# A two-layer graph network with expert layers, second stage: expert groups of two node tiles instead of four, two experts to a step, a fourth gather buffer, and inverse square roots computed on VectorE

## What is computed

```python
x = x + gnn0(layernorm(x))       # h = x @ weight_l, gathered over 100000 edges, weighted, summed by dst
x = x + experts0(layernorm(x))   # 8 experts, all applied, weighted by a softmax gate
x = x + gnn1(layernorm(x))
x = x + experts1(layernorm(x))   # 32 experts, the best one applied
# experts0, for each expert e:
h = relu(bn(x @ W1[e] + b1)); h = relu(bn(h @ W2[e] + b2)); y = h @ Wo[e] + bo; out += w[e] * y
# layernorm: (x - mean) / sqrt(var + 1e-5);  bn: g * (h - m) / sqrt(v + 1e-3) + be
```

## Time and profile before

| | |
|---|---|
| median of three executions | 2962.04 us |
| the profiled execution | 2958.48 us, its span 2956.5 us |
| TensorE busy | 2599.4 us (88%) |
| VectorE busy | 2167.4 us (73%) |
| ScalarE busy | 1565.7 us (53%) |
| GpSimd busy | 1957.5 us (66%) |
| second stage, slot 26 to 195 (577 to 1690 us) | 1113 us |
| second stage after the last edges (1690 to 1828 us) | about 138 us |

### The profile page before, as it was taken

The page is one execution under the profiler, slowest core; times in us unless marked ns, Lnnn a source line. Parts: engine busy times, 40 slices in busy tenths (PEclk is TensorE's granted clock), DMA queues, the critical chain, the costliest instruction groups (busy, mean ns, idle before and its releaser), DMA issues. The chain is left out here.

```text
span 2956.5 us, 54481 instructions
## 1 busy us (share of the span) xinstructions
PE 2599.4 (88%) x19092; PEld 2420.7 (82%) x19092; DVE 2167.4 (73%) x5110; ACT 1565.7 (53%) x3295; POOL 1957.5 (66%) x1696
## 2 busy tenths in 40 slices
PE   5799935799999999999999994599999999999999
PEld 5799825788888888888888873489999999999999
DVE  8898836577787777777878754767777777777773
ACT  4477636788888888888888762111212112121212
POOL 0355557777777877777777501877777777777770
PEclk9999956799999999999999997689999999999999
DMA  2133454332333333233233203788888888888880
GB/s 74 6 82 77 93 137 144 91 97 78 109 108 91 99 108 110 79 107 110 78 115 108 80 1 114 212 205 214 204 215 214 212 208 215 213 213 209 212 212 24
DMA packets 241962, 390.31 MB, mean 132 GB/s; under 512 B 43642, under 2 KB 115218, under 8 KB 241426
## 3 DMA queue, kind: packets, MB, share of 16 engines
q0 software_dynamic: 163072, 310.24, 41.1%
q1 hardware_dynamic: 78324, 74.90, 8.0%
q10 hardware_dynamic: 288, 1.61, 0.1%
HBM read 343.43 MB, written 43.19 MB: 131 GB/s over the span
## 5 line engine op out<-in xcount | busy, mean ns | idle before, releaser
L1409 POOL DMA_INDIRECT f_got<-h_tab,list_cols x784 | 981.1, 1251 | 291.0 <-issue 219.1
L2121 POOL DMA_INDIRECT n_got<-h_tab,edge_cols x784 | 806.5, 1029 | 238.5 <-issue 227.6
L1690 DVE TENSOR_TENSOR f_hlo<-edge_cols,f_hhi 128x1024 fp32r<-128x1024 f32 (+1 forms) x208 | 242.0, 1163 | 294.3 <-ACT f_hhi L1498 294.1
L1585 PE MATMUL bank<-f_mhi,f_hot 128*128 128x256 f32 x1168 | 329.0, 311 | 131.2 <-DVE f_mlo L1684 131.1
L1468 ACT ACTIVATE f_got<-f_got,list_cols 128x256 f32<-128x256 f32 x784 | 333.9, 497 | 145.6 <-DMA f_got<-h_tab,list_cols 145.1
L2185 ACT ACTIVATE n_hrh<-bank 128x512 fp32r<-128x512 f32 x196 | 116.9, 597 | 535.6 <-PE bank L2254 535.6
L1585 PEld LDWEIGHTS bank<-f_mhi,f_hot 128*128 128x128 f32 x1168 | 247.6, 212 | 148.0 <-issue 143.8
L1493 ACT ACTIVATE edge_cols<-bank,f_shf,f_scl 128x512 f32<-128x512 f32 (+1 forms) x416 | 295.1, 743 | 106.9 <-PE bank L1400 76.7
L2232 PE MATMUL bank<-n_got,n_hot_h 128*128 128x256 f32 x784 | 242.2, 309 | 99.4 <-DMA n_got<-h_tab,edge_cols 59.0
L1586 PE MATMUL bank<-f_mlo,f_hot 128*128 128x256 f32 x1168 | 320.3, 304 | 0.0
L400 POOL DMA_INDIRECT list<-runs,off_i x98 | 158.0, 1612 | 215.2 <-DVE off_i L759 99.0
(11 more groups left out here) (331 smaller groups left out, 7833.0 us busy)
## 6 DMA issues: line engine op xcount, KB each, us to landing
f_got<-h_tab,list_cols POOLq DMA_INDIRECT x784
n_got<-h_tab,edge_cols POOLq DMA_INDIRECT x784, 3.8
n_rows<-acc_tab SPq DMA_DIRECT2D x24, 256.0 KB, 4.7
out_rows<-n_rows SPq DMA_DIRECT2D x24, 256.0 KB, 3.7
h_tab<-acc SPq DMA_DIRECT2D x37, 128.0 KB, 3.5
edge_cols<-in_w SPq DMA_DIRECT2D x16, 256.0 KB, 2.8
acc<-in_x SPq DMA_DIRECT2D x4, 896.0 KB, 7.9
h_tab<-hbuf SPq DMA_DIRECT2D x7, 512.0 KB
```

What stands on the lines that cost most here:

```text
L1409: nc.gpsimd.indirect_dma_start(got[:, s % RING0, u, :], None, h_tab[0], bass.IndirectOffsetOnAxis(gidx0[:, s * U + u:s * U + u + 1], 0), b ...
L1585: nc.tensor.matmul(tile_bank(t), lhs, mhi[:, s % 2, u, :], start=begins, stop=False)
L1690: nc.vector.tensor_tensor(hlo[l][:, :, 0:w], rl[:, :, 0:w], hhi[l][:, :, 0:w].bitcast(F32), ALU.subtract).then_inc(s_lo[l], 1)
L2121: nc.gpsimd.indirect_dma_start(got[:, s % RING, u, :], None, h_tab[1], bass.IndirectOffsetOnAxis(gidx[:, s * U + u:s * U + u + 1], 0), bou ...
```

## The change

Groups get two tiles (`GS` = 2, 256 columns; group 0 still one), and a step takes as many experts as fill 512 columns: two (four for group 0). `layer` then issues 48 matmuls of 256 columns where it issued 24 of 512, each relu pair is four activations of 256 columns, and `hhi`, `hlo` and `add_out` keep their sizes. Four steps make a group, so that a group comes every 8 slots. Group 1 begins in slot 18, the steps of group 0 in slots 10 and 12, and the number of steps falls from 104 to 98. The rows of groups lie in six places instead of three, `rl` is two buffers, and the rows after the experts have places of their own (`before4`), which removes some waits. `RING0` is 4. The roots on ScalarE go; VectorE computes the inverse root from a first guess by bit shift and three rounds, 11 small dependent instructions where it had 5 (`inverse_root`). The same is done for the roots of the batch norm at the start.

```diff
-GS = 4
+GS = 2
+ROW_SETS = 6
...
-RING0 = 3
+RING0 = 4
...
+SEED = float(0x5f3759df)
+ROOT_STEPS = 11
...
-            xraw, rl = (edge_cols[:, b * F * W4:(b + 1) * F * W4].rearrange("p (f n) -> p f n", f=F) for b in range(2))
+            xraw, rl0 = (edge_cols[:, b * F * W4:(b + 1) * F * W4].rearrange("p (f n) -> p f n", f=F) for b in range(2))
+            rl = (rl0, sb3("rl1", [P, F, W4]))
...
+            def experts_of(g):
+                return W4 // (width(g) * P)
+
+            CUM = tuple(itertools.accumulate((EXPERTS0 // experts_of(g) for g in range(NG)), initial=0))
+            STEPS = CUM[NG]
+            GROUP_OF_STEP = [g for g in range(NG) for _ in range(CUM[g], CUM[g + 1])]
...
-                FFN.append(max(READY[g] + 5, FFN[-1] + 2 * EXPERTS0 if g else 0))
-            STEPS = NG * EXPERTS0
+                FFN.append(max(READY[g] + 5, FFN[-1] + 2 * (CUM[g] - CUM[g - 1]) if g else 0))
 
             def begin(n):
-                return FFN[n // EXPERTS0] + n % EXPERTS0 * 2
+                g = GROUP_OF_STEP[n]
+                return FFN[g] + (n - CUM[g]) * 2
+
+            def step_experts(n):
+
+                g = GROUP_OF_STEP[n]
+                per = experts_of(g)
+                return g, range((n - CUM[g]) * per, (n - CUM[g]) * per + per)
+
+            def columns(g, i):
+                return slice(i * width(g) * P, (i + 1) * width(g) * P)
...
-            DONE = [FFN[g] + 2 * EXPERTS0 + 2 for g in range(NG)]
-            NORM4 = [DONE[g] + (1 if g == NG - 1 else 2) for g in range(NG)]
+            DONE = [FFN[g] + 2 * (CUM[g + 1] - CUM[g]) + 2 for g in range(NG)]
+            NORM4 = [DONE[g] + (1 if g == NG - 1 else 3) for g in range(NG)]
             BASE = [DONE[g] + (1 if g == NG - 1 else 6) for g in range(NG)]
+            BIAS = [READY[g] + (10 if g == NG - 2 else 9) for g in range(NG)]
             UPPER = [n + 1 for n in NORM4]
             LOWER = [NORM4[g] + (1 if g == NG - 1 else 2) for g in range(NG)]
...
-                pairs = range((width(g) + 1) // 2)
-                for j in pairs:
-                    USES.append((READY[g] + 2 + j, "turn", g, j))
-                    USES.append((READY[g] + (9, 15)[j], "bias", g, j))
+                USES.append((READY[g] + 2, "turn", g, 0))
+                USES.append((BIAS[g], "bias", g, 0))
...
-                return store[g % 3][:, k, :]
+                return group_rows(g)[:, k, :]
 
             def group_rows(g, a=0, b=None):
-                return store[g % 3][:, a:width(g) if b is None else b, :]
+                at = g % 2 * GS
+                return store[g // 2 % 3][:, at + a:at + (width(g) if b is None else b), :]
 
 
 
             def before(k):
-                return (acc[:, 4, :], acc[:, 5, :], acc[:, 6, :], part[:, 6, :])[k]
-
-            def behind(j, w=2):
-                return (part, xn)[j][:, 4:4 + w, :]
+                return acc[:, 4 + k, :]
+
+            def before4(k):
+                return (acc[:, 6, :], part[:, 6, :])[k]
+
+            def behind(k):
+                return part[:, 4 + k, :]
...
-                    if l:
-                        act.wait_ge(s_lo[0], n + 1)
-                    elif n:
-                        act.wait_ge(s_lo[1], n)
+                    if n:
+                        act.wait_ge(s_lo[l], n)
                     i = 4 * n + 2 * l
                     for m in range(F):
                         act.wait_ge(s_mm[l], 2 * n + m + 1)
-                        nc.scalar.activation(rl[:, m, 0:w], bank[(i + m) % 3][:, 0:w], ACT.Relu,
-                                             bias=shf[:, l, e, m:m + 1], scale=scl[:, l, e, m:m + 1]).then_inc(s_relu, 1)
+                        for j, e in enumerate(experts):
+                            last = nc.scalar.activation(rl[l][:, m, columns(g, j)], bank[(i + m) % 3][:, columns(g, j)],
+                                                        ACT.Relu, bias=shf[:, l, e, m:m + 1], scale=scl[:, l, e, m:m + 1])
+                        last.then_inc(s_relu, 1)
                     act.wait_ge(s_relu, i + 2)
                     if n:
                         act.wait_ge(s_mm[l + 1], (2 - l) * n)
-                    nc.scalar.activation(hhi[l][:, :, 0:w], rl[:, :, 0:w], ACT.Copy).then_inc(s_hi[l], 1)
+                    nc.scalar.activation(hhi[l][:, :, :], rl[l][:, :, :], ACT.Copy).then_inc(s_hi[l], 1)
...
-                    if s - 1 in READY:
-                        g = READY.index(s - 1)
-                        t, w = tile(g, 0), width(g)
-                        act.wait_ge(s_var, t + w)
-                        nc.scalar.activation(scale[:, t:t + w], var[:, t:t + w], ACT.Sqrt).then_inc(s_sd, 1)
...
+                        for j, e in enumerate(experts):
+                            if g == 0 and m == 0:
+                                pe.wait_ge(s_wlo, 3 * e + l + 1)
+                            at = columns(g, j if l else 0)
+                            hi_x, lo_x = (hhi[0], hlo[0]) if l else (xhi, xlo)
+                            for f in range(F):
+                                last = three(bank[i % 3][:, columns(g, j)],
+                                             whi[l][:, e, f, m * P:(m + 1) * P], wlo[l][:, e, f, m * P:(m + 1) * P],
+                                             hi_x[:, f, at], lo_x[:, f, at], f == 0, f == F - 1)
...
+                    for j, e in enumerate(experts):
+                        if g == 0:
+                            pe.wait_ge(s_wlo, 3 * e + 3)
+                        for k in range(width(g)):
+                            o = j * width(g) + k
+                            for f in range(F):
+                                last = three(out_tile(o), hhi[1][:, f, o * P:(o + 1) * P], hlo[1][:, f, o * P:(o + 1) * P],
+                                             whi[2][:, e, f, :], wlo[2][:, e, f, :], f == 0, f == F - 1)
...
+                    for j, e in enumerate(experts):
+                        if e:
+                            dve.wait_ge(s_out, OUT_TILES * n + j * width(g))
+                        for k in range(width(g)):
+                            nc.vector.scalar_tensor_tensor(row(g, k), out_tile(j * width(g) + k), gate[:, g % 2, k, e:e + 1],
+                                                           row(g, k), ALU.mult, ALU.add).then_inc(s_out, 1)
+
+                def inverse_root(r, v, x, counter, base):
+
+                    bits, seed = v.bitcast(I32), r.bitcast(I32)
+                    nc.vector.tensor_scalar(x.bitcast(I32), bits, 1, None, ALU.arith_shift_right).then_inc(counter, 1)
+                    dve.wait_ge(counter, base + 1)
+                    nc.vector.tensor_scalar(seed, x.bitcast(I32), -1.0, SEED, ALU.mult, ALU.add).then_inc(counter, 1)
+                    for i in range(3):
+                        dve.wait_ge(counter, base + 3 * i + 2)
+                        nc.vector.tensor_tensor(x, r, r, ALU.mult).then_inc(counter, 1)
+                        dve.wait_ge(counter, base + 3 * i + 3)
+                        nc.vector.scalar_tensor_tensor(x, x, -0.5, v, ALU.mult, ALU.mult).then_inc(counter, 1)
+                        dve.wait_ge(counter, base + 3 * i + 4)
+                        nc.vector.scalar_tensor_tensor(r, x, 1.5, r, ALU.add, ALU.mult).then_inc(counter, 1)
+                    dve.wait_ge(counter, base + ROOT_STEPS)
...
-                        dve.wait_ge(s_sd, g + 1)
-                        newton(t, w, s_newton, 5 * g)
+                        dve.wait_ge(s_var, t + w)
+                        newton(t, w, s_newton, ROOT_STEPS * g)
                         if g:
-                            dve.wait_ge(s_made, USE_NO["turn", g - 1, (width(g - 1) - 1) // 2] + 1)
-                        split = [h for h in range(NG) if LOWER[h] <= s]
-                        if split:
-                            dve.wait_ge(s_hst, 16 * HSTORES[split[-1] + 1])
+                            dve.wait_ge(s_made, USE_NO["turn", g - 1, 0] + 1)
...
-                        dve.wait_ge(s_sd4, g + 1)
-                        newton(t, w, s_newton4, 5 * g)
+                        dve.wait_ge(s_var4, g + 1)
+                        newton(t, w, s_newton4, ROOT_STEPS * g)
                         if g:
                             dve.wait_ge(s_hst, 16 * HSTORES[g])
-                        turns = [h for h in range(NG) if READY[h] + 1 <= s]
-                        dve.wait_ge(s_made, USE_NO["turn", turns[-1], (width(turns[-1]) - 1) // 2] + 1)
                         for k in range(w):
-                            nc.vector.tensor_scalar(before(k), row(g, k), mean[:, t + k, 0:1],
+                            nc.vector.tensor_scalar(before4(k), row(g, k), mean[:, t + k, 0:1],
```

138 lines of the change are left out of this document (40 added, 98 removed).

## The result

The changed kernel takes 2957.61 us (median of 20 runs), the kernel before 2965.99 in as many: ratio **0.9972, interval 0.9962 to 0.9982, 8.4 us faster**. Forecast were 2978 us and, as the likeliest, slower by over 0.2%. The time lies in the range, the sign is wrong. The profiled execution of the changed kernel took 2956.42 us (span 2954.5), 1.2 less than its median; that of the kernel before (2958.48, span 2956.5) lies 7.5 under its own. So the two traces show only part of the gain: the gathers of the third stage start at 1833.16 us instead of 1837.29, 4.1 us earlier.

The account below looks back on a forecast made before the run. No single engine but a ring of TensorE, ScalarE and VectorE, just under the gathers' floor of 100.6 us a period. 49.7 + 5.8 + 7.4 - 41.1 - 2.9 - 3 = +15.9 gave 2978 us; range 2908 to 3022.

Parts of the forecast that it names:

- the period: 16 slots of the steps with edges: 105.5 us now, 110.2 us forecast, by waits +1.5, matmuls +1.5, clock +1.7.
- Matmuls: Two layers of a step on TensorE, 256 columns instead of 512: 5.74 us instead of 5.55, +1.5 us a period.
- Late gathers: 3.3 of the 8.7 us of TensorE's waits a period; would go with the fourth buffer or without it.
- Waits: TensorE's `edges` waiting for `mlo`: 2.0 and 3.0 us in 8 slots, 10.2 a period against 8.7, so +1.5.
- The walk: Slots 6 to 9 (modulo 8) followed by instruction durations on TensorE, ScalarE and VectorE: `mlo` done at 6.1 and 21.9 us.
- Clock: TensorE's granted clock falls to 0.50 behind long waits: two falls a period instead of one, +1.7 us.
- rival (b): TensorE's clock falls at each of four long waits in 16 slots, +3.4 us a period: 3016 us, chance 0.13.
- Slots 10 to 26: Group 0's two steps with four experts each, +7.4 us, and slots 18 to 26, scaled from the period, +5.8.
- After the edges: Expert steps behind the last edges: 7 instead of 11, -41.1 us; freer relus -2.9; smaller last group -3.
- Rival (a): VectorE's idle time swallows the normalisation blocks, late gathers go, no added clock fall: 103.7 us a period, 2906 us, chance 0.33.
- Rival (c): VectorE's small instructions are dearer: a root takes 3.3 us, the period grows by 3.6: 3018 us, chance 0.12.
- (d): The roots' table loads stay on ScalarE because another function needs a table; the forecast's time, no chance of its own.

Follow-up runs that it names:

- `mlo` first: Changed kernel with the lower half of the messages (mlo) issued on VectorE ahead of layer 1's lower half in every slot; 2905.3 us, ratio 0.9809 to the kernel before.
- the longer root: Changed kernel with a fourth round in each root on VectorE; ratio 1.0129 to the kernel before, 46 us more than the changed kernel.

## Why the prediction was wrong

**The step that failed is the period**: 110.2 us forecast, 107.7 measured, that is 4.7 us more than before against 2.5. Of its terms, the waits were put at +1.5 and measured +0.1, the clock was put at +1.7 and measured +1.1, and the matmuls +1.5 and +1.3. The waits were too long because VectorE's work between the `mlo` of slots 7 and 9 was given 15.8 us and takes 15.2; and the falls of the clock were added to waits that they shorten.

- *Matmuls*, +1.5 us a period: +1.3 measured, as all of TensorE's work without the clock. Right.
- *Late gathers*, 3.3 of 8.7 us: 3.3 in the kernel before with four buffers, 2.6 of them idle time. Right in kind, 0.7 too high as a wait. "With the fourth buffer or without it" was wrong: with three the changed kernel takes 0.9 us a period more.
- *Relus.* Most relus of 256 columns start 0.45 us apart, as forecast. Pieces of both kinds (matmuls and relus) cost 3.1 us a period in the kernel before.
- *Waits.* The walk gave 10.2 us a period; the idle time is 8.4. Slot 7 was right (2.15 against 2.0). From the `mlo` of slot 7 to that of slot 9 the walk had 21.9 - 6.1 = 15.8 us, the rows show 1231.25 - 1216.06 = 15.2. Its steps hold one by one; a block is 0.26 us shorter than forecast, and two of them are 0.5 of the 0.6 us. TensorE in turn was ready 0.25 us later than the walk had it, so that slot 9 waits 2.1 and not 3.0 where the clock stayed up. The root has 2.19 us instead of 2.4: all eleven instructions start 0.20 us apart, the shift and the guess too, for which I had taken 0.30. These two took 0.16 to 0.17 us on integers; the `tensor_scalar` of four elements from which I had scaled took 0.33. The number of elements is not the reason, as one of two elements in the run with the roots on ScalarE took 0.36 in one block and 0.17 in the next:

```profile
1052.09 0.36 DVE L1743 TENSOR_SCALAR f_nwt<-f_nwt 128x2 f32<-128x2 f32 x1
...
1056.80 0.17 DVE L1743 TENSOR_SCALAR f_nwt<-f_nwt 128x2 f32<-128x2 f32 x1
```

- *Clock.* Predicted as one fall more, +1.7; measured +1.1. Before has 1.3 falls a period, not one, and after 2.0, as forecast for after. A fall takes 1.7 us of TensorE's busy time; in these rows the 16 matmuls of `edges` in slot 7 take 3.6 us (1054.56 to 1058.16) instead of 2.1. The last two rows are the next `edges` in slots 9 and 11.

```profile
1054.56 0.55 PE L1586 MATMUL bank<-f_mhi,f_hot 128*128 128x256 f32 x1 [2.15 <-DVE f_mlo L1687]
1054.91 0.41 PE L1587 MATMUL bank<-f_mlo,f_hot 128*128 128x256 f32 x1
...
1057.88 0.28 PE L1587 MATMUL bank<-f_mlo,f_hot 128*128 128x256 f32 x1
...
1069.72 0.36 PE L1586 MATMUL bank<-f_mhi,f_hot 128*128 128x256 f32 x1 [0.65 <-DVE f_mlo L1687]
...
1082.57 0.36 PE L1586 MATMUL bank<-f_mhi,f_hot 128*128 128x256 f32 x1 [1.24 <-DVE f_mlo L1687]
```
```profile
1054.50:1056.50 2.00, 1.95 (x9) 1.98 (x10) 1.23 (x2) 2.00 (x4) 1.70 (x2) 0.50 0.21 61
1056.50:1058.50 2.00, 2.00 (x14) 2.00 (x14) 1.66 (x11) 1.52 (x5) 1.70 (x2) 0.66 0.19 53
1058.50:1060.50 2.00, 2.00 (x19) 2.00 (x18) 1.96 (x5) 0.82 (x1) 1.39 (x3) 1.00 0.27 82
```

Behind 2.15 us of idle time TensorE runs at 0.50, the level of 1.2 GHz, and then again at 2.4. But from slot 7 to slot 9 it takes 1069.72 - 1054.56 = 15.2 us, as in the rows without this fall: `mlo` of slot 9 comes when VectorE is ready, and TensorE, 1.5 us later, waits 0.65 us instead of 2.13. **This fall costs nothing**, it is taken out of a wait; the prediction added falls and waits as if they could not overlap. Each of 19 stretches from one slot 7 to the next has one fall. In 8 it stands behind slot 7, and the stretch takes 53.7 us; in 11 behind slot 9, and it takes 54.0, since there TensorE needs 13.1 us to the `edges` of slot 11, where in the other case it has to wait for their `mlo` until 12.85. Only where no such wait follows is the fall paid nearly whole: 51.3 against 52.7 us with `mlo` first.

The forecast of two falls a period for this kernel held, so rival (b), a fall behind each of four long waits, is refuted; its own sign, a granted clock under 0.95, stayed away (0.97). The Trainium skill ("TensorE: Matmul & The Clock Gate", HAM oscillation) warns that idle gaps pay the slow start each time. The runs agree in part. A wait of 2.15 us in slot 7 is followed by a fall in 8 of 19 stretches, and with `mlo` first one of 2.1 us in slot 9 in 4 of 19; with the roots on ScalarE, where the waits are mostly 1.7, 1.2 and 0.7 us, there are 0.5 falls a period. What decides where one comes is not shown.

- *Slots 10 to 26.* Together +11.6 against +13.2, but the division was wrong, and the near agreement is luck. Group 0 cost +13.0: its first layer came behind 5.01 us of idle time and ran from 486.2 to 496.7 us at half clock throughout, 10.5 us instead of the 5.1 forecast; a later one (506.93 to 512.46) took 5.5. These 5.4 us are the miss: the forecast had every layer at full clock. The eight slots behind it gained 1.4 where they were put at +5.8; I scaled them from the later period. There the clock decides: by the sum of busy time x (1 - granted clock) it took 9.9 us of these slots before, when they carried narrow steps, and takes 1.6 after, while in slots 10 to 18 it took 9.1 before and 9.4 after. The slots from 18 to 26, before and then after:

```profile
527.58:576.83 49.25, 36.52 (x228) 35.49 (x228) 25.63 (x45) 33.01 (x68) 39.23 (x33) 0.79 0.29 86
```
```profile
541.64:589.48 47.84, 43.01 (x341) 42.19 (x342) 37.69 (x75) 43.29 (x81) 38.65 (x31) 0.96 0.32 98
```

And the first layer of group 0:

```profile
486.19 0.48 PE L1414 MATMUL bank<-f_xhi,f_whi 128*128 128x128 f32 x1 [5.01 <-DVE f_xlo L1802]
```
```profile
486.00:491.00 5.00, 4.81 (x23) 4.81 (x23) 3.50 (x7) 2.33 (x5) 4.00 (x4) 0.50 0.29 89
491.00:497.00 6.00, 6.00 (x29) 6.00 (x29) 0.00 (x0) 1.77 (x5) 4.78 (x5) 0.50 0.35 99
```

- *After the edges.* -43.7 against -47.0: 7 steps of 10.1 us ((1810.73 - 1740.02) / 7) instead of 9.9, which is 1.4 of the 3.3 us. The free relus brought under 0.2 us a step and not 0.4. From the last `outputs` to the third stage it takes 22.4 us instead of 24.4, 2 us less where 3 were forecast. The last `outputs` pays a wait of 3.46 us, which is not new (3.21 before):

```profile
1740.02 0.39 PE L1414 MATMUL bank<-f_whi,f_hhi 128*128 128x256 f32 x1 [0.42 <-DVE f_hlo L1692]
...
1810.73 0.39 PE L1414 MATMUL bank<-f_whi,f_hhi 128*128 128x256 f32 x1 [3.46 <-DVE f_hlo L1692]
```

Rival (a) is refuted by its time (2906 us against 2957.6) and, for blocks that grow, by the longer root, though the sign was its own: the time fell not because VectorE swallows the blocks but because the loss in the middle (26.9 us) was smaller than the gain behind it (43.7). Rival (c) had the wrong direction: the root took 2.19 us, not 3.3. Of (d) nothing is seen: from 600 to 1680 us the kernel before has 21 table loads, the changed one none. The single changes nearly add up to the period: 105.3 - 3.3 (buffer) + 3.1 (pieces) + 2.2 (roots) = 107.3 against 107.7. That is luck in part: the buffer's 3.3 is from the kernel before, and in the changed kernel it is worth 0.9. Groups of two tiles by themselves, with all else as before, were not run.

## What to carry to other kernels

Where a forecast is the small difference of two large terms (here +27 and -44 us), the chance of its sign hangs on a few tenths of a microsecond in a block that is repeated 42 times: ask for the slope, time per microsecond of the block, before trusting the sum. Waits and falls of TensorE's clock are not to be added without a look at what waits next: a fall ahead of another wait was free here (53.7 against 54.0 us in 8 slots), a fall with none behind it cost 1.4 us. Shortening several long waits a little (roots on ScalarE) took most falls away, and that was nearly its whole gain. And before an order of work is changed, look for the cheap places: a buffer more, or an instruction that moves into a neighbour's idle time, brought 27 and 48 us, where the whole regrouping brought 8; but the second did so only with two relu buffers, and in the kernel before, with one, it cost 35 us. And a slope measured by making a block longer is not the slope of making it shorter: 0.6 us more a block cost 46 us, 1.2 us less brought nothing on the chips where it was tried.
